# Retention heads in two 64-row halves of TensorE, taken in pairs, with row tile 6 moved to VectorE

## The reference, cut to what matters

```python
scores = jnp.einsum('bhtd,bhsd->bhts', q, k) * mask
denom = jnp.clip(jnp.abs(scores).sum(-1, keepdims=True), 1.0, 50000.0)
scores = scores / denom
ret = jnp.einsum('bhts,bhsv->bthv', scores, v)
ret = ret * jax.lax.rsqrt(jnp.mean(ret * ret, axis=-1, keepdims=True) + EPS)
gated = (x @ W_g + b_g) * y
```

## Time and profile before

| what | value |
|---|---|
| median of 3 runs | 2383.02 us (2376.03 to 2388.97) |
| profiled execution | 2386.77 us, span 2385.0 us |
| busy share of the span | PE 81%, PEld 44%, DVE 70%, ACT 58%, POOL 19% |
| ACT passes, L1920 | 176, mean 952 ns, 167.5 us; 46.8 us idle before them |
| DVE reductions, L1955 | 224, mean 515 ns, 109.0 us; 61.2 us idle before them |
| PE banks for ACT, L1873 | 352, mean 423 ns, 118.4 us |
| PE banks for DVE, L1887 | 224, mean 347 ns, 72.1 us |

### The profile page before, as it was taken

One profiled execution on the slowest core, in us unless ns is written; L12 is line 12 of the kernel. 1 busy time (PEld: TensorE's weight loads), 2 busy tenths in 40 slices (PEclk: granted clock), 3 DMA queues, 4 the chain that ended last, 5 costly groups with the idle time before them and its releaser, 6 DMA issues. The chain is left out here.

```text
span 2385.0 us, 38939 instructions
## 1 busy us (share of the span) xinstructions
PE 1936.0 (81%) x12970; PEld 1046.3 (44%) x12970; DVE 1677.1 (70%) x4201; ACT 1374.0 (58%) x2027; POOL 455.2 (19%) x816
## 2 busy tenths in 40 slices
PE   5899899975699974687899899957557999999839
PEld 3433333333477753464333333337334333333338
DVE  6688798747466777567798898632696897888423
ACT  4257667865378865435367677832543466677712
POOL 4010120110245430220101110133000010211233
PEclk8599999996899986897699999978865799999959
DMA  7342020001201000006032020014024402200034
GB/s 218 81 72 37 3 38 2 2 33 32 79 38 40 38 18 1 1 1 174 17 59 38 3 38 2 2 47 176 25 59 118 72 13 26 38 2 2 2 106 159
DMA packets 47527, 113.89 MB, mean 48 GB/s; under 512 B 11952, under 2 KB 21426, under 8 KB 43144
## 3 DMA queue, kind: packets, MB, share of 16 engines
q1 hardware_dynamic: 40308, 96.84, 17.2%
q0 software_dynamic: 5088, 11.24, 1.5%
q10 hardware_dynamic: 1964, 3.70, 0.4%
HBM read 62.39 MB, written 32.64 MB: 40 GB/s over the span
## 5 line engine op out<-in xcount | busy, mean ns | idle before, releaser
L1124 ACT ACTIVATE probs<-score 128x1024 f32<-128x1024 f32 x960 | 822.8, 897 | 429.1 <-PE score L1223 423.1
L1294 DVE TENSOR_REDUCE max_part<-stat 128x1 f32<-128x512 f32 x1152 | 724.7, 682 | 94.0 <-PE stat L1175 86.2
L1237 PE MATMUL pv<-probs,v_ones 128*9 128x512 f32 (+3 forms) x3840 | 458.4, 551 | 0.6 <-ACT out_turned L1117 0.6
L1291 DVE CUSTOM_DVE_ANT_0 masked_scores<-stat,mask_row 128x128 f32<-128x128 f32 (+3 forms) x768 | 346.8, 487 | 145.3 <-PE stat L1175 142.2
L1175 PE MATMUL stat<-first_group_k,first_group_q 64*128 64x512 f32 (+2 forms) x960 | 364.2, 496 | 41.5 <-PEq L708 16.1
L1175 PE MATMUL stat<-group_k,group_q 64*128 64x512 f32 (+2 forms) x960 | 337.4, 407 | 16.2 <-DVE max_part L1294 7.7
L1175 PEld LDWEIGHTS stat<-first_group_k,first_group_q 64*128 64x128 f32 x960 | 176.7, 215 | 288.3 <-DVE max_part L1294 174.6
L1175 PEld LDWEIGHTS stat<-group_k,group_q 64*128 64x128 f32 x960 | 157.8, 185 | 279.2 <-DVE max_part L1294 162.1
L1223 PE MATMUL score<-first_group_q,first_group_k 64*128 64x512 f32 x960 | 251.3, 423 | 32.0 <-ACT probs L1124 19.6
L1223 PE MATMUL score<-group_q,group_k 64*128 64x512 f32 x960 | 229.8, 418 | 40.4 <-ACT probs L1124 31.3
L1920 ACT ACTIVATE abs_act_ps<-abs_act_ps 128x1024 f32<-128x1024 f32 (+3 forms) x176 | 167.5, 952 | 46.8 <-PE abs_act_ps L1873 43.2
(11 more groups left out here) (369 smaller groups left out, 2488.7 us busy)
## 6 DMA issues: line engine op xcount, KB each, us to landing
tile_wv<-expert_wv SPq DMA_DIRECT2D x38, 512.0 KB, 3.2
q_parts<-early_parts_t SPq DMA_DIRECT2D x21, 512.0 KB, 3.8
k_parts<-early_parts_t SPq DMA_DIRECT2D x12, 512.0 KB, 4.7
group_k<-k_parts SPq DMA_DIRECT2D x24, 256.0 KB, 11.9
group_q<-q_parts SPq DMA_DIRECT2D x24, 256.0 KB, 18.2
head_q<-q_parts SPq DMA_DIRECT2D x32, 128.0 KB
head_k<-k_parts SPq DMA_DIRECT2D x32, 128.0 KB
first_group_q<-pad_rows SPq DMA_DIRECT2D x6, 512.0 KB, 5.6
```

What stands on the lines that cost most here:

```text
L1124: nc.scalar.activation(probs[:, n % PSLOTS, :, 0:width], sc[m % 2][:, :, 0:width], ACT.Exp, scale=scale).then_inc(slot_read.sem, 1)
L1237: last = nc.tensor.matmul(acc[32 * h:32 * h + D + 1, f:BANK], v9[:, kt, g * HG + h, :], probs[:, (2 * t + h // 2) % PSLOTS, h % 2, 0:BANK ...
L1291: nc.vector.tensor_tensor_reduce(masked[:, at % 2, 0:width], ring[n % RBANKS][:, 0:width], w["mask_row"][:, BANK - width:BANK], 1.0, NEG, ...
L1294: nc.vector.reduce_max(into, ring[n % RBANKS][:], AX.X).then_inc(stat_used.sem, 1)
```

## The change

Two heads are loaded as a pair, the even one into rows 0 to 31 of the tiles and the odd one into rows 64 to 95; rows 32 to 63 and 96 to 127 are zero. The two buffers now hold two pairs, so a pair's load is eight DMAs on one semaphore, and it starts when PE has finished the pair two earlier. PE goes through 16 seats as before. In a seat ACT's banks come from one head of the pair and DVE's banks from the other, by matmuls in 64-row halves; in the pair's second seat the two change places. Each bank for ACT is an item of PE's order by itself, so banks for ACT and for DVE alternate one by one. Row tile 6 leaves `ACTU`, which falls from 11 to 10 units, and becomes three 256-wide units of DVE, so `NV` rises from 18 to 21. The places of the pieces, the transposes and the read-out keep their numbers in DVE's units. POOL and DVE take the head numbers 1, 0, 3, 2, and so on. PE's loop covers four seats and runs three times, after four seats written out.

```diff
-    ACTU = [(i, 0, min(i * P, LONG)) for i in range(5, NT)]
+    SPLIT = 6
+    ACTU = [(i, 0, min(i * P, LONG)) for i in range(5, NT) if i != SPLIT]
...
+        if i == SPLIT:
+            DVEU += [(i, n * 2 * P, 2 * P, n) for n in range(SPLIT // 2)]
         while at < i * P:
-            DVEU.append((i, at, min(BANK, i * P - at)))
+            DVEU.append((i, at, min(BANK, i * P - at), 1 + (at // BANK) % 2))
...
-        PADDED = (slice(KROWS, 2 * KROWS), slice(2 * KROWS, P))
-        NL = 2 * PARTS * 16
+        PADDED = (slice(KROWS, HROWS), slice(HROWS + KROWS, P))
+        NL = 2 * 2 * PARTS * 16
+        TURNS = H // 4
...
+        abanks = [(m, b) for m, (i, at, width) in enumerate(ACTU) for b in range(0, width, BANK)]
         order = []
         for n in range(NV):
-            order += [("a", m) for m in range(n * NA // NV, (n + 1) * NA // NV)]
+            order += [("a", bank) for bank in abanks[n * len(abanks) // NV:(n + 1) * len(abanks) // NV]]
             order.append(("d", n))
...
-                def body(h, par, first=False):
+                def load_pair(p, buf, first=False):
                     if not first:
-                        sp.wait_ge(a_full.sem, a_full.at(h * NA - NA))
-                        sp.wait_ge(d_full.sem, d_full.at(h * NV - NV))
...
+                        sp.wait_ge(a_full.sem, a_full.at(p * 2 * NA - 2 * NA))
+                        sp.wait_ge(d_full.sem, d_full.at(p * 2 * NV - 2 * NV))
+                    for half in range(2):
+                        for a in range(PARTS):
+                            at = slice(half * HROWS + a * PARTS * D, half * HROWS + (a + 1) * PARTS * D)
+                            sp.dma_start(qm[at, buf, :], bcast(q_rows[p * 2 + half, a], 0, PARTS)).then_inc(loaded[buf].sem, 16)
+                            sp.dma_start(km[at, buf, :], k_rows[p * 2 + half]).then_inc(loaded[buf].sem, 16)
...
-                def body(h, turn, par, first=False, second=False):
-                    pe.wait_ge(loaded[par].sem, loaded[par].at(turn * NL + NL))
+                def body(h, turn, seat, first=False, second=False):
+
+                    buf, par = seat // 2, seat % 2
+                    here, other = (slice(HROWS * half, HROWS * half + HROWS) for half in (par, 1 - par))
+                    if par == 0:
+                        pe.wait_ge(loaded[buf].sem, loaded[buf].at(turn * NL + NL))
                     for kind, n in order:
                         if kind == "a":
...
+                            m, b = n
+                            slot = (seat * NA + m) % 2
+                            if b == 0 and (not first or m >= 2):
+                                pe.wait_ge(a_used.sem, a_used.at(h * NA + (m - 1)))
+                            i, at, width = ACTU[m]
+                            ins = nc.tensor.matmul(a_ps[slot][:, b:min(b + BANK, width)], rounded(qm[here, buf, i * P:(i + 1) * P]),
+                                                   rounded(km[here, buf, at + b:at + min(b + BANK, width)]), start=True, stop=True,
+                                                   tile_position=(here.start, 0))
+                            if b + BANK >= width:
+                                ins.then_inc(a_full.sem, 1)
                             continue
...
-                            ins = nc.tensor.matmul(out[:, 0:width], rounded(qm[:, par, i * P:(i + 1) * P]), rounded(km[:, par, at:at + width]), start=True, stop=True)
+                            i, at, width, _ = DVEU[n - ND]
+                            ins = nc.tensor.matmul(out[:, 0:width], rounded(qm[other, buf, i * P:(i + 1) * P]), rounded(km[other, buf, at:at + width]),
+                                                   start=True, stop=True, tile_position=(other.start, 0))
...
-                body(0, 0, 0, first=True)
-                body(1, 0, 1, second=True)
-                with pe.Fori(1, H // 2) as n:
-                    for par in range(2):
-                        body(2 * n + par, n, par)
+                for seat in range(4):
+                    body(seat, 0, seat, first=seat == 0, second=seat == 1)
+                with pe.Fori(1, TURNS) as n:
+                    for seat in range(4):
+                        body(4 * n + seat, n, seat)
```

More of the change, by code:

```diff
@@ L1782, in _ @@
             def _(sp):
-                def body(h, par, first=False):
+                def load_pair(p, buf, first=False):
                     if not first:
-                        sp.wait_ge(a_full.sem, a_full.at(h * NA - NA))
-                        sp.wait_ge(d_full.sem, d_full.at(h * NV - NV))
[L1787 to L1790, removed]
-                wait_parts(sp, stored)
-                body(0, 0, first=True)
-                body(1, 1, first=True)
-                with sp.Fori(1, H // 2) as n:
-                    for par in range(2):
-                        body(2 * n + par, par)
+                        sp.wait_ge(a_full.sem, a_full.at(p * 2 * NA - 2 * NA))
[5 more added lines that the diff above has]
+                            sp.dma_start(km[at, buf, :], k_rows[p * 2 + half]).then_inc(loaded[buf].sem, 16)
+                wait_parts(sp, stored)
+                load_pair(0, 0, first=True)
+                load_pair(1, 1, first=True)
+                with sp.Fori(1, TURNS) as n:
+                    for buf in range(2):
+                        load_pair(2 * n + buf, buf)
             @block.gpsimd
@@ L1814, in _, with gate_head, body @@
                 pool.wait_ge(cleared.sem, cleared.at(5))
-                def gate_head(h):
+                def gate_head(h, head):
                     pool.wait_ge(o_used.sem, o_used.at(2 * h + 1))
-                    g, r = (t[:, :, bass.ds(h * VD, VD)] for t in (gate, ret))
+                    g, r = (t[:, :, bass.ds(head * VD, VD)] for t in (gate, ret))
                     nc.gpsimd.tensor_tensor(g, g, r, ALU.mult).then_inc(gated.sem, 1)
-                def body(h, par, first=False):
+                def body(h, head, par, first=False):
                     if not first:
@@ L1934, in _, with take_out, body @@
                 dve.wait_ge(cleared.sem, cleared.at(1))
-                def take_out(h):
+                def take_out(h, head):
                     dve.wait_ge(o_turned.sem, o_turned.at(h + 1))
                     o = o_ps[:].rearrange("p (t e) -> p t e", e=OW)
-                    r = ret[:, :, bass.ds(h * VD, VD)]
+                    r = ret[:, :, bass.ds(head * VD, VD)]
                     nc.vector.tensor_tensor(r, o[:, :, 0:VD], r, ALU.add).then_inc(o_used.sem, 1)
-                    nc.vector.tensor_copy(diag[:, bass.ds(h, 1), :], o[:, :, VD]).then_inc(o_used.sem, 1)
-                def body(h, par, first=False, first_two=False):
+                    nc.vector.tensor_copy(diag[:, bass.ds(head, 1), :], o[:, :, VD]).then_inc(o_used.sem, 1)
+                def body(h, head, before, par, first=False, first_two=False):
                     for n in range(NV):
@@ L1952, in body @@
                         else:
-                            i, at, width = DVEU[n - ND]
-                            slot = 1 + (at // BANK) % 2
-                            nc.vector.tensor_reduce(part[:, bass.ds(h, 1), i, slot:slot + 1], d_ps[n % DRING][:, 0:width], AX.X, ALU.add,
+                            i, at, width, slot = DVEU[n - ND]
+                            nc.vector.tensor_reduce(part[:, bass.ds(head, 1), i, slot:slot + 1], d_ps[n % DRING][:, 0:width], AX.X, ALU.add,
                                                     apply_absolute_value=True).then_inc(d_used.sem, 1)
                         if n == READ_AT and not first:
-                            take_out(h - 1)
-                body(0, 0, first=True, first_two=True)
-                body(1, 1, first_two=True)
+                            take_out(h - 1, before)
+                body(0, 1, None, 0, first=True, first_two=True)
+                body(1, 0, 1, 1, first_two=True)
                 with dve.Fori(1, H // 2) as n:
                     for par in range(2):
-                        body(2 * n + par, par)
-                take_out(H - 1)
+                        body(2 * n + par, 2 * n + 1 - par, 2 * n - 2 + 3 * par, par)
+                take_out(H - 1, H - 2)
         for par in range(2):
-            loaded[par].done(NL * H // 2)
+            loaded[par].done(NL * TURNS)
         cleared.done(5)
```

28 lines of the change are left out of this document (9 added, 19 removed).

## The result

The changed kernel takes **2446.74 us** (median of 4 runs, 2435.4 to 2461.11), against 2382.81 for the kernel before beside it: a ratio of **1.0272, 95% interval 1.0219 to 1.0324**. It is slower by 64 us where no change was forecast. The profiled execution took 2461.11 us (span 2459.3), 14 above its median; its rows are read for where the time lies, not for the last ten microseconds.

The account below looks back on a forecast made before the run. PE was taken as the pace, by waits in its written-out order rather than its columns. Heads -6.6, steady loads -1.3 and start +9.9 summed to +2.0 us: 2385 us, no measurable change, range 2366 to 2404 us.

Parts of the forecast that it names:

- The step that failed: Retention heads: 64-row matmuls as in the softmax stretch keep PE's clock at 1.00, so the clock was priced at nothing.
- The head of 13.0 us: Retention stage: ACT work 10.47, waits 2.39, transposes 0.1 per head, against 13.41 before; 16 x 0.41 = 6.6 us saved.
- The changes of form: Full-height transposes between 64-row matmuls: two more changes a head, taken as 0.1 us, between 0 and 0.5.
- Row tile 6: Moved to DVE: ACT loses a 0.81 us pass per head; DVE rises from 9.5 to 10.8 us, costed at nothing.
- The loads: Stage start waits for eight loads instead of four, 9.9 us lost; in the steady part pairing saves 1.3 us.
- B: Rival: the halves do not overlap in the retention heads; head 14.1 us, sum +20, 2403 us; chance 0.17.
- A: Rival: the array really doubles, waits at the own-part pieces vanish; head 11.3 us, sum -25, 2358 us; chance 0.18.

## Why the prediction was wrong

**The step that failed** is one sentence: "The softmax stretch holds clock 1.00 with such matmuls, so I price the clock at nothing." The granted clock is 0.61, and at 0.50 a head takes 18.4 us. That sentence reads the earlier trace rows as a stretch of such matmuls, which it is only by half. Its commonest matmuls from 142 to 519 us, by form:

```profile
L1237 PE MATMUL pv<-probs,v_ones 128*9 128x512 f32 x848 | 110.8, 595 | 0.2 <-ACT out_turned L1117 0.2
L1175 PE MATMUL stat<-group_k,group_q 64*128 64x512 f32 x224 | 84.2, 440 | 2.9 <-DVE max_part L1294 0.8 <-DVE max_part L1291 0.4
```

In all, 1208 of the stretch's 2406 matmuls are those of L1237, over all 128 rows, and 1125 are 64 rows high. The pace differs too. In the earlier trace rows the halves are worked pair upon pair, 0.34 us apart; in a retention head a pair comes each 1.01 us at the pieces. Which of the two differences holds the clock in the softmax layer, no run tells. For the retention heads the runs name two causes that act together: 64 rows in place of 128 (1.00 becomes 0.50 ahead of any piece), and changes of form (22 of them harmless to the clock at full height; with 64 rows six fewer bring 0.61 to 0.74, forty more 1.00 to 0.50). More 64-row matmuls bring the clock back. A stretch of another stage, with another mix of matmuls, was taken for a bound of this one.

**The head of 13.0 us** was never put to the test alone, as no head of the changed kernel ran through at 1.00. In the stretches that did, pairs start together and a piece's slot takes 1.01 us where 0.97 was used. With the clock held by added matmuls a head took 13.3 or 13.43 us, that work included: hardly less than the 13.41 to 13.55 of before. So with the clock the loss in the heads goes, and what is left to gain is small; how much of these heads the added work costs is open.

**The changes of form** were priced in time alone: at the pieces within their slots (0.97, measured 1.01), at the transposes at 0.1 a head (two changes at the 0.14 us measured at full height are 0.28, inside the bound of 0.5). As terms of time they were small, as taken. Their other price, the clock, was missed.

**Row tile 6**, whose move was to spare ACT 0.81 us a head and cost nothing, did not pay at full height. With pairs, moving it made the head 0.26 us longer (13.0 against 12.74; the pairs stand one and two slots later), and together with the order bank by bank 0.6 longer (14.15 against 13.55).

**The loads** were right, in size and in kind: 9.9 us forecast, 10.3 measured, and no later wait for a load. With nothing gained in the heads they now add to the loss.

**The rivals.** B had the sign and said it would decide from 13.6 us a head on, but by another mechanism (no overlap) and with 14.1 us; the halves did overlap. A did not come: no steady head went under 12.1 us, not even with the clock held. None of the cases held a lower clock, and the range ended at 2404.

## What to carry to other kernels

A kernel that is paced by TensorE at 2.4 GHz has the clock among its terms: whoever halves the height of its matmuls must ask whether the clock stands, and no stretch of another stage answers that unless its matmuls are of the same forms and follow each other in the same way. Read the granted clock by stretch before any wait; and before splitting the array, try what needs no split: here own-part pieces sent two by two and loads cut over more steps together gave 0.6%, where the split cost 2.7%.

## What was not expected of the hardware

- PE was marked busy for 210 of 210 us with the clock at 0.50, in three of the runs. The Trainium skill's TensorE: Matmul & The Clock Gate (HAM oscillation — how this bites in real kernels) ties a swinging clock to PE standing idle for data. No such wait stands in these rows, so here the clock is lost in another way.
- Work that computes nothing made a kernel faster: 2446.74 to 2413.59 us.
- A change of form costs 0.14 us at the upper clock, the small matmul that makes it included. The Trainium skill's TensorEngine Tiling (Key Properties) has the engine drained at each change of tiling mode; that price is in keeping with it, though no row shows the drain itself. Among 64-row matmuls forty more changes a head went with the clock's fall from 1.00 to 0.50.
- The first matmul came 14.0 us after the first load was issued instead of 22.7, by the order of a transfer's loops alone. The first issue for k took 0.42 us instead of 0.68, that for q 0.82 instead of 0.74.
